# A graph-attention layer on one core: the first stage redone, with twelve sets of adjacency rows issued during the projection

## The chip, the cores and the metric

The kernel runs on one core of a Trainium2 chip. The time is device microseconds (us) of one execution, as the median of several runs. One further execution was profiled; rows and stretches below are from that one. TensorE (PE) multiplies, VectorE (DVE), ScalarE (ACT) and GpSimd (POOL) do elementwise work, SyncE (SP) only issues DMAs. PEld is TensorE's weight load.

## What is computed

```python
h  = relu(layernorm(x))                 # x: 8192 x 256, f32
Wh = h @ W + b                          # 8192 x 256
e  = leaky_relu((Wh @ a1)[:, None] + (Wh @ a2)[None, :], 0.2)
att = softmax(where(adj > 0, e, -9e15), axis=1)   # adj: 8192 x 8192, int32
out = x + att @ Wh
```

With s = Wh a1 and t = Wh a2, the exponential of leaky_relu(s_i + t_j) is the greater of two products of a row factor and a column factor. So the weight of a pair is max(q_i * r_j, sigma) times a column factor c_j that is multiplied into Wh, and the adjacency limits it from above (`min` with a number made of the adjacency bits). The softmax denominator is one more column of Wh.

## The kernel before

**Tiling.** The 8192 rows of x are 64 blocks of 128. The output is made in NS = 8 rows of R = 1,024 output rows ("row 0" to "row 7"). Each row takes all 8192 columns in NK = 32 units of two blocks. Eight PSUM banks `acc` hold the 8 x 128 output rows, and a unit is 2 x 8 x 3 fp16 products of 128 x 257 (high times high, high times low, low times high parts; `part`, L636).

**First stage.** SyncE loads the parameters and then x into `x_in` in four groups of 16 blocks (L194). For each group VectorE takes statistics (`stats`, L408; aggregation L414), adds eps (L416), ScalarE takes the square root (L272), and VectorE inverts (L418) and makes the shift (L419). Then, block by block: ScalarE normalises into a two-buffer `h` (`normalise`, L280), TensorE transposes it (L604), ScalarE copies the transpose out of PSUM (`copy_hT`, L287), TensorE projects (L612; two more columns of W, made of W times a at L395, give s and t), VectorE adds the bias and stores Wh with s and t in the tile `X` (`add_bias`, L426), and GpSimd sums Wh over the blocks (`add_wh`, L244). In between GpSimd issues the first 8 sets of adjacency rows, a set after every fourth block.

**Adjacency.** A set is four DMAs of a quadrant of 32 partitions (`load_adj`, L251, on GpSimd's queue, int32 cast to uint8). There are R8 = 12 slots; set n waits for the transpose of set n - 12 (`s_T`). VectorE turns a set with one transpose (L457); 8 sets are a chunk of 8 units.

**Between projection and row 0.** VectorE takes the largest and smallest t (L460 to L463), GpSimd reduces them over the partitions (L258) and then goes on to sets 8 and later; VectorE makes exponents (L468 to L475), ScalarE the exponentials (L347 to L351), VectorE scales q (L484). SyncE stores q to HBM in four DMAs, waits for all four, and loads row 0 of q into every partition:

```python
            sp.wait_ge(s_qn, 1)
            for q in range(NQ):
                sp.dma_start(q_store[q], ...).then_inc(s_qst, 16)
            sp.wait_ge(s_qst, 16 * NQ)
            load_q(0)
            sp.wait_ge(s_mean, 1)
```

**A unit of the main part.** ScalarE makes two products q * r_j (`product`, L323), VectorE takes max and min (`weights`, L508), ScalarE the high parts in fp16 (`high`, L338), VectorE the low parts (`low`, L515), TensorE multiplies. Four units are in flight (RING = 4). In row 0 alone, ScalarE and VectorE also split each block of Wh, scaled by c_j, into high and low halves (`x_high`, L344; `x_low`, L521), in place in `X`. ScalarE does four products of row 0 before the first high part. `first_units` waits for two units, then goes bank by bank, opening each bank with a product with the column mean of Wh (L647). At the end of a row `finish` (L529, L532) divides and adds x, and SyncE stores.

The order on each engine is written out by hand, and every engine runs its own list in order; semaphores tie them together.

Of the kernel before, what the change touches and what calls it, by code (L numbers as in the profile page):

```python
# [12 lines left out]
RMAX = bass.bass_isa.ReduceOp.max  # L13
RADD = bass.bass_isa.ReduceOp.add

P = 128
# [8 lines left out]
TINY = 2.0 ** -100  # L25


def gat_layer(nc, x, adj, W_w, W_b, a, out):

# [25 lines left out]
    KF = F // P  # L55
    XG = Y
    AHEAD = 2
# [11 lines left out]
    with ctx:  # L69
# [6 lines left out]

        X = sb("X", [P, NB + AHEAD, F2], F32)
        X16 = X[:, :, :].bitcast(F16).rearrange("p b (k f) -> p b k f", k=2)
        wh_s_t = X[:, AHEAD:AHEAD + NB, :]
        wh = X[:, AHEAD:AHEAD + NB, 0:F]  # L80
        wh_one = X[:, AHEAD:AHEAD + NB, 0:F1]
        s_in = X[:, AHEAD:AHEAD + NB, F]
        t_in = X[:, AHEAD:AHEAD + NB, F1]

# [5 lines left out]
        r_j = sb("r_j", [P, NB], F32)  # L90
        c_j = sb("c_j", [P, NB], F32)
        sigma = sb("sigma", [P, 1], F32)
# [12 lines left out]
        h = xr[:, 0, 0:2, :]  # L105
        hT = xr[:, 0, 2:4, :]
        prod = h[:, 0, :]
        a_row = hT
# [3 lines left out]
        wh_sum = xr[:, 1, 0:2, :]  # L112
        small = xr[:, 1, 2:4, :].rearrange("p k f -> p (k f)")
        st = small[:, 0:96].rearrange("p (n v) -> p n v", n=XG)
        mv = small[:, 96:128].rearrange("p (n v) -> p n v", n=XG)
        rstd = small[:, 128:192]
        shift = small[:, 192:256]
        ones = small[:, 256:384]
        mean_hi = small[:, 384:512].bitcast(F16)
# [5 lines left out]
        sc = sb("sc", [P, 16], F32)  # L125
# [3 lines left out]
        ps_wh = [acc[:, 2, :], acc[:, 3, :]]  # L129
        ps_tot = acc[:, 4, :]  # L130

        s_par = sem("params_loaded")
        s_x = [sem(f"x_loaded{k}") for k in range(NB // XG)]
        s_rows = [sem(f"adj_loaded{k}") for k in range(R8)]
        s_qst = sem("q_stored")
        s_q = sem("q_loaded")
        s_xr = [sem(f"x_rows_loaded{k}") for k in range(2)]
        s_out = [sem(f"out_stored{k}") for k in range(2)]

        s_ident = sem("ident_step")  # L140
        s_wsq = sem("w_squares_in_partition")
        s_wsq_all = sem("w_squares_summed")
        s_wnorm = sem("w_norm_ready")
        s_var = sem("variance_ready")
        s_std = sem("std_ready")
        s_norm = sem("norm_factors_ready")
        s_ext = sem("extremes_ready")
        s_top = sem("extremes_of_all_ready")
# [3 lines left out]
        s_c = sem("column_factors_ready")  # L152
        s_tot = sem("sum_wh_in_psum")
        s_mean = sem("mean_wh_ready")
        s_chain = sem("vector_chain")
        s_bn = sem("bn_step")

        s_h = sem("h_ready")
        s_ht = sem("h_transposed")
        s_hT = sem("hT_ready")  # L160
        s_whp = sem("wh_in_psum")
        s_wh = sem("wh_ready")
        s_sum = sem("wh_summed")
        s_xhi = sem("x_hi_ready")
        s_X = sem("X_ready")
# [18 lines left out]
        def _(sp):  # L184
            for k in range(KF):
                sp.dma_start(Wx[:, k, 0:F], W_w[k * P:(k + 1) * P, :]).then_inc(s_par, 16)
            sp.dma_start(bias[:, 0:F], W_b.rearrange("(o f) -> o f", o=1).broadcast_to([P, F])).then_inc(s_par, 16)
# [3 lines left out]
            for k in range(NC):  # L191
                xk = x_in[:, k * Y:(k + 1) * Y, :].rearrange("p (w e) f -> p w (e f)", e=4)
                for q in range(NQ):
                    sp.dma_start(xk[QP * q:QP * (q + 1)], x_cols[q, k]).then_inc(s_x[k], 16)  # L194
# [9 lines left out]

            sp.wait_ge(s_qn, 1)
            for q in range(NQ):
# [22 lines left out]
        @block.gpsimd  # L229
        def _(pool):  # L230
            nc.gpsimd.memset(ident[:, :], 0.0).then_inc(s_ident, 1)
            pool.wait_ge(s_ident, 1)
            nc.gpsimd.affine_select(out=ident[:, :], in_=ident[:, :], compare_op=ALU.not_equal, fill=1.0, base=0,
                                    pattern=[[-1, P]], channel_multiplier=1).then_inc(s_ident, 1)
            pool.wait_ge(s_wsq, 1)
            nc.gpsimd.partition_all_reduce(sc[:, 1:2], sc[:, 0:1], P, RADD).then_inc(s_wsq_all, 1)

            def add_wh(b, k, first):
                pool.wait_ge(s_wh, b + 1)
                if first:  # L240
                    nc.gpsimd.tensor_copy(wh_sum[:, k, :], wh[:, b, :]).then_inc(s_sum, 1)
                else:
                    pool.wait_ge(s_sum, b - 1)
                    nc.gpsimd.tensor_tensor(wh_sum[:, k, :], wh_sum[:, k, :], wh[:, b, :], ALU.add).then_inc(s_sum, 1)  # L244
            def load_adj(n):

                if n >= R8:
                    pool.wait_ge(s_T, n - R8 + 1)
                s, k, m = n // NSET, n % NSET // SETS, n % SETS
                for q in range(NQ):  # L250
                    pool.dma_start(rows8[QP * q:QP * (q + 1), n % R8], adj_v[s, m, k, q]).then_inc(s_rows[n % R8], 16)  # L251

            for b in range(NB):
                add_wh(b, b % 2, b < 2)
                if b >= SETS and b % 4 == 0 and b // 4 - 2 < SETS:
                    load_adj(b // 4 - 2)
            pool.wait_ge(s_ext, 1)
            nc.gpsimd.partition_all_reduce(top[:, :], ext[:, :], P, RMAX).then_inc(s_top, 1)  # L258
            for n in range(SETS, NSET * NS):
                load_adj(n)  # L260

        @block.scalar
        def _(act):
            act.wait_ge(s_par, 16 * (KF + 3))
            nc.scalar.activation(h, Wx[:, :, 0:F], ACT.Square, accum_out=sc[:, 0:1]).then_inc(s_wsq, 1)
            act.wait_ge(s_wsq_all, 1)
            nc.scalar.activation(sc[:, 2:3], sc[:, 1:2], ACT.Sqrt, scale=float(F)).then_inc(s_wnorm, 1)

            def std(k):
                act.wait_ge(s_var, k + 1)  # L270
                v = rstd[:, k * XG:(k + 1) * XG]
                nc.scalar.activation(v, v, ACT.Sqrt).then_inc(s_std, 1)  # L272

            std(0)
            act.wait_ge(s_norm, 1)

            def normalise(b, k, first):
                if not first:
                    act.wait_ge(s_ht, b - 1)
                nc.scalar.activation(h[:, k, :], x_in[:, b, :], ACT.Relu, scale=rstd[:, bass.ds(b, 1)],  # L280
                                     bias=shift[:, bass.ds(b, 1)]).then_inc(s_h, 1)

            def copy_hT(b, k, first):
                act.wait_ge(s_ht, b + 1)
                if not first:
                    act.wait_ge(s_whp, b - 1)
# [417 lines left out]
```

## Time and profile before

| | |
|---|---|
| median of 3 runs | 1554.79 us (1554.2 to 1555.71) |
| the profiled execution | 1553.04 us, its span 1551.1 |
| TensorE, busy share of the span | 93% |
| VectorE | 92% |
| ScalarE | 72% |
| GpSimd | 38% |
| granted TensorE clock, mean | 0.982 |

The span is the time from the first to the last instruction in the profile. A row of a timeline gives the start, the time, the engine, the line in the kernel, the operation, what it writes and reads, and how many were merged (x4). "Idle before" names what released the engine. A granted clock of 1.00 is 2.4 GHz, 0.50 is 1.2 GHz. The clock is given per stretch. Matmuls are pipelined, so a busy TensorE isn't a TensorE at its peak.

### The profile page before, as it was taken

The numbers are of one execution on the slowest core, as the hardware profiler recorded it, in microseconds if no ns is written. First come the engines' busy times: TensorE is split into PE (matmuls) and PEld (weight loads), VectorE is DVE, ScalarE is ACT, GpSimd is POOL, SyncE is SP. The second block draws the span as 40 slices with busy tenths as digits, with TensorE's granted clock in tenths as the row PEclk, the third lists the DMA queues.
The fourth block names the chain that finished last, engine by engine and source line by source line (L and its number), as shares of the span: only waits on it lengthen the run. The fifth ranks groups of instructions, "written<-read, shape, count | busy, mean of one in ns | idle before, by whom it ended". The sixth has DMA issues, their size and how long they took to land.

```text
span 1551.1 us, 30326 instructions
## 1 busy us (share of the span) xinstructions
PE 1448.3 (93%) x12740; PEld 1258.0 (81%) x12740; DVE 1425.4 (92%) x1155; ACT 1110.9 (72%) x975; POOL 593.7 (38%) x1096
## 2 busy tenths in 40 slices
PE   2880899979999999999999999999999999999998
PEld 2760787768888888888888888888888888888887
DVE  4654999999999999999999999999999999999994
ACT  3664788877777677768777777768777777767771
POOL 0866433334444344334434343434343434423000
PEclk9995899999999999999999999999999999999999
DMA  9719866668776777778777877778767877676000
GB/s 195 80 14 118 65 44 48 44 60 103 56 55 59 100 56 52 52 84 81 52 52 63 100 54 53 60 99 57 54 49 62 103 55 53 49 97 50 1 1 28
DMA packets 170768, 99.07 MB, mean 64 GB/s; under 512 B 19472, under 2 KB 167568, under 8 KB 170640
## 3 DMA queue, kind: packets, MB, share of 16 engines
q0 software_dynamic: 147456, 67.17, 61.2%
q1 hardware_dynamic: 23184, 30.05, 7.1%
q8 instruction: 97, 1.59, 0.4%
q14 instruction: 31, 0.25, 0.1%
HBM read 290.06 MB, written 8.42 MB: 192 GB/s over the span
## 4 chain that ended last, share of the span: by engine, by line
PE 82%; DVE 12%; issue 2%; DMA 2%; ACT 1%; SPq 0%; DVEq 0%; POOL 0%; ACTq 0%; POOLq 0%
PE acc L636 77%; DVE work L515 4%; PE acc L612 3%; DVE work L508 3%; DVE X L521 1%; DMA work<-in_x 1%; PE acc L604 1%; DMA q_rows<-q_j 1%; DVE adj_cols L457 1%; DVE xr L408 1%; ACT work L323 1%; PE acc L647 0%; DMA work<-q_rows 0%; DVE xr L414 0%; ACT work L338 0%
## 5 line engine op out<-in xcount | busy, mean ns | idle before, releaser
L636 PE MATMUL acc<-X,work 128*128 128x257 f16 x12288 | 1372.6, 273 | 12.9 <-DVE work L515 12.9
L636 PEld LDWEIGHTS acc<-X,work 128*128 128x128 f16 x12288 | 1189.4, 97 | 188.8 <-DVE work L515 16.8
L251 POOL DMA_DIRECT2D adj_rows<-in_adj x1024 | 550.8, 545 | 776.0 <-DVE adj_cols L457 752.5
L338 ACT ACTIVATE work<-work 128x2048 f16<-128x2048 f32 x256 | 487.6, 1907 | 276.7 <-PE acc L636 274.0
L508 DVE SCALAR_TENSOR_TENSOR work<-work,sigma,adj_cols 128x2048 f32<-128x2048 f32 x256 | 594.6, 2323 | 20.8 <-issue 17.3
L515 DVE SCALAR_TENSOR_TENSOR work<-work 128x2048 f16<-128x2048 f32 x256 | 584.9, 2285 | 29.3 <-ACT work L338 29.2
L323 ACT ACTIVATE work<-work,r_j 128x1024 f32<-128x1024 f32 x256 | 278.1, 1134 | 28.3 <-DMA work<-q_rows 17.9
L323 ACT ACTIVATE work<-q_odd,r_j 128x1024 f32<-128x1024 f32 x256 | 278.5, 1135 | 23.3 <-DVE work L515 23.3
L457 DVE STREAM_TRANSPOSE adj_cols<-adj_rows 128x512 int32<-128x512 int32 x256 | 176.0, 699 | 0.0
L612 PE MATMUL acc<-q_odd,xr 128*128 128x258 f32 x256 | 68.8, 393 | 9.0 <-DVE X L426 9.0
L647 PE MATMUL acc<-mean_wh,tiny 128*128 128x257 f16 x64 | 17.7, 276 | 47.1 <-DVE work L515 46.5
L426 DVE TENSOR_TENSOR X<-acc,q_odd 128x258 f32<-128x258 f32 (+1 forms) x64 | 26.9, 423 | 34.4 <-PE acc L612 32.3
L612 PEld LDWEIGHTS acc<-q_odd,xr 128*128 128x128 f32 x256 | 45.2, 197 | 14.0 <-DVE X L426 9.7
L344 ACT ACTIVATE X<-X,c_j 128x257 f16<-128x257 f32 x64 | 29.1, 504 | 30.8 <-DVE X L521 29.1
L604 PE MATMUL acc<-q_odd,xr 128*128 128x128 f32 x128 | 25.2, 282 | 27.2 <-ACT xr L280 27.2
L244 POOL TENSOR_TENSOR xr<-xr,X 128x256 f32<-128x256 f32 x62 | 41.2, 683 | 19.9 <-DVE X L426 19.7
L604 PEld LDWEIGHTS acc<-q_odd,xr 128*128 128x128 f32 x128 | 18.3, 145 | 34.2 <-issue 27.5
L647 PEld LDWEIGHTS acc<-mean_wh,tiny 128*128 128x128 bf16 x64 | 6.2, 96 | 48.7 <-issue 47.7
L280 ACT ACTIVATE xr<-work,xr 128x256 f32 (+1 forms) x64 | 38.3, 600 | 6.0 <-issue 5.2
L287 ACT COPY xr<-acc 128x256 f32<-128x256 f32 x64 | 23.7, 370 | 16.4 <-PE acc L604 12.1
L521 DVE SCALAR_TENSOR_TENSOR X<-X,c_j 128x257 f16<-128x257 f32 x64 | 28.0, 480 | 0.0
L532 DVE SCALAR_TENSOR_TENSOR xr<-acc,rden,xr 128x256 f32<-128x256 f32 x64 | 26.5, 477 | 0.6
(60 smaller groups left out, 54.0 us busy)
## 6 DMA issues: line engine op xcount, KB each, us to landing
adj_rows<-in_adj POOLq DMA_DIRECT2D x1024, 64.0 KB, 3.7
work<-in_x SPq DMA_DIRECT2D x16, 512.0 KB, 21.4
xr<-in_x SPq DMA_DIRECT2D x16, 512.0 KB, 4.0
out<-xr SPq DMA_DIRECT2D x16, 512.0 KB, 3.8
work<-q_rows SPq DMA_DIRECT2D x4, 512.0 KB, 5.7
q_odd<-q_rows SPq DMA_DIRECT2D x4, 512.0 KB, 5.4
q_odd<-in_L_gnn_W_w SPq DMA_DIRECT2D x2, 128.0 KB, 2.1
xr<-in_L_gnn_a SPq DMA_DIRECT2D x2, 128.0 KB, 6.1
```

The costliest lines, as they stand in the source:

```text
L244: nc.gpsimd.tensor_tensor(wh_sum[:, k, :], wh_sum[:, k, :], wh[:, b, :], ALU.add).then_inc(s_sum, 1)
L251: pool.dma_start(rows8[QP * q:QP * (q + 1), n % R8], adj_v[s, m, k, q]).then_inc(s_rows[n % R8], 16)
L280: nc.scalar.activation(h[:, k, :], x_in[:, b, :], ACT.Relu, scale=rstd[:, bass.ds(b, 1)], bias=shift[:, bass.ds(b, 1)]).then_inc(s_h, 1)
L323: ins = nc.scalar.mul(Wt[:, i % RING, e, :], q_bc[s % 2], r_j[:, 2 * k + e:2 * k + e + 1])
L338: nc.scalar.mul(Et[:, at:at + 2, 0, :], Wt[:, i % RING], SCALE).then_inc(s_H, 1)
L457: nc.vector.transpose(rows.rearrange("p w (q r) -> p q w r", q=SQ), rows8[:, n % R8].bitcast(I32).rearrange("p q (w c) -> p q w c", w=CW)) ...
L508: nc.vector.scalar_tensor_tensor(out=slot, in0=slot, scalar=sigma[:, 0:1], in1=edges, op0=ALU.max, op1=ALU.min).then_inc(s_M, 1)
L515: nc.vector.scalar_tensor_tensor(out=Et[:, at:at + 2, 1, :], in0=Wt[:, i % RING], scalar=SCALE, in1=Et[:, at:at + 2, 0, :], op0=ALU.mult, ...
L521: nc.vector.scalar_tensor_tensor(out=X16[:, b, 1, 0:F1], in0=wh_one[:, b, :], scalar=c_j[:, b:b + 1], in1=X16[:, b, 0, 0:F1], op0=ALU.mult ...
L604: ins = nc.tensor.transpose(ps_hT[k][:, c * P:(c + 1) * P], h[:, k, c * P:(c + 1) * P], ident)
L612: ins = nc.tensor.matmul(ps_wh[k][:, 0:F2], hT[:, k, c * P:(c + 1) * P], Wx[:, c, :], start=(c == 0), stop=(c == KF - 1))
L636: return nc.tensor.matmul(acc[:, m, 0:F1], Et[:, 2 * (k % RING) + e, 1 if n == 2 else 0, m * P:(m + 1) * P], X16[:, 2 * k + e, 1 if n == 1 ...
```

## The change

The diff rewrites the first stage and leaves the unit of the main part as it was.

- x comes in seven groups (4, 4, 8, 8, 8, 16, 16 blocks), the first ahead of the parameters. The inverse square root is made on VectorE, from the bits of the number and three rounds of Newton's method. The steps are dealt out over the pairs of blocks (`STATS_AT`, `norms`).
- `normalise` works in place in `x_in`. The odd blocks' transposes are copied out by VectorE, the even ones' by ScalarE.
- Wh is no longer stored. It stays in one of six PSUM banks, and `x_high` and `x_low` split it from there during the projection. Since the largest t isn't known yet, each pair of blocks is scaled by its own greater t (`greater_t`, `column_exps`, `scale_columns`); r_j and sigma (now one value for each pair) are corrected for that later.
- The bias is left out of Wh and is added to x's rows by an accumulating DMA (`add_bias` on GpSimd's queue, 16 in all), before `finish` uses them.
- GpSimd adds h instead of Wh, and TensorE makes the mean of Wh from the sum. The reductions over partitions are products on TensorE.
- All twelve sets of adjacency rows that have a slot are issued during the projection, a quadrant after each add from block 8 on. Four sets are transposed in the last four pairs.
- SyncE stores the first half of the first quarter of q, loads row 0 of q, and stores the rest behind it.
- Row 0: ScalarE begins with two products instead of four, and TensorE starts after one unit.

The diff, cut to its core:

```diff
+    GROUPS = [(0, 0, 1, 0), (0, 1, 2, 4), (0, 2, 4, 8), (1, 0, 2, Y), (1, 2, 4, Y + 8), (2, 0, 4, 2 * Y), (3, 0, 4, 3 * Y)]
+    STATS_AT = [None, None, (0, 2), (2, 2), (5, 2), (8, 4), (14, 4)]
...
             sp.wait_ge(s_qn, 1)
-            for q in range(NQ):
-                sp.dma_start(q_store[q], q_j[QP * q:QP * (q + 1), :].rearrange("p (z e) -> p z e", e=4)).then_inc(s_qst, 16)
+            store_q(0, 0, NZ // 2, s_q0)
+            sp.wait_ge(s_q0, 16)
+            load_q(0)
+            store_q(0, NZ // 2, NZ, s_qst)
+            for q in range(1, NQ):
+                store_q(q, 0, NZ, s_qst)
             sp.wait_ge(s_qst, 16 * NQ)
-            load_q(0)
+            sp.wait_ge(s_X, NB)
             sp.wait_ge(s_mean, 1)
...
+            for b in range(1, NB):
+                add_h(b)
+                if EARLY <= b < EARLY + NQ * R8:
+                    load_quadrant(*divmod(b - EARLY, NQ))
+            for n in range(R8, NSET * NS):
                 load_adj(n)
+                if n % NSET == 2 * R8 + 3:
+                    for half in range(2):
+                        add_bias(n // NSET, half)
...
+            for p in range(PAIRS + 1):
+                if p >= 2:
+                    x_high(2 * p - 4)
+                    x_high(2 * p - 3)
+                if 2 * p + 3 < NB:
+                    normalise(2 * p + 3)
+                if p >= 1:
+                    column_exps(p - 1)
+                if 2 * p + 2 < NB:
+                    copy_hT(2 * p + 2)
+                if 2 * p + 4 < NB:
+                    normalise(2 * p + 4)
...
-            for i in range(RING):
-                product(0, i)
+            product(0, 0)
+            product(0, 1)
             high(0, 0)
+            product(0, 2)
+            high(0, 1)
+            product(0, 3)
+            product(0, 4)
...
+            def root(g):
+                b, n = of_group(g)
+                a, y = newt[:, 0:n], rstd[:, b:b + n]
+                step(nc.vector.scalar_tensor_tensor(out=a, in0=y, scalar=-0.5, in1=y, op0=ALU.mult, op1=ALU.mult))
+                step(nc.vector.tensor_tensor(a, a, var[:, 0:n], ALU.mult))
+                step(nc.vector.scalar_tensor_tensor(out=y, in0=a, scalar=1.5, in1=y, op0=ALU.add, op1=ALU.mult))
...
+            def norms(p, place):
+                for g in range(2, len(GROUPS)):
+                    at, turns = STATS_AT[g]
+                    n = p - at
+                    if place == 0 and 0 <= n < turns:
+                        stats(g, 4 * n, 4 * n + 4)
+                    if place == 0 and n == turns:
+                        variance(g)
+                    if place == 1 and n == turns:
+                        guess(g)
+                        root(g)
+                    if place == 2 and n == turns:
+                        root(g)
+                    if place == 3 and n == turns:
+                        root(g)
+                        shifts(g)
+
+            def pair(p):
+                copy_hT(2 * p + 1)
+                if p >= 1:
+                    read_s_t(p - 1)
+                norms(p, 0)
+                if p >= 1:
+                    greater_t(p - 1)
+                norms(p, 1)
+                if p >= 2:
+                    x_low(2 * p - 4)
+                norms(p, 2)
+                if p >= 2:
+                    x_low(2 * p - 3)
+                norms(p, 3)
+                if p >= 1:
+                    scale_columns(p - 1)
...
+            first_groups()
+            for p in range(PAIRS):
+                pair(p)
+                if p == 0:
+                    bounds()
+                if p >= PAIRS - TURNED:
+                    transpose(0, p - PAIRS + TURNED)
...
+            def project(b):
+                k = b % 2
+                pe.wait_ge(s_hT[k], b // 2 + 1)
+                if b >= WH:
+                    pe.wait_ge(s_X, b - WH + 1)
...
+            for m in range(M):
+                start(m)
+            unit(0, 0)
+            unit(0, 1).then_inc(s_pe, 1)
```

`first_groups` does the statistics and factors of groups 0 and 1 and the four products of W with a. `variance` is the aggregation and the addition of eps, `guess` one operation on the bits, `shifts` one more. `bounds` makes the power of two that scales all columns, from the norm of W.

## Rows read from the trace of the kernel before

**Rows 1.** Stretches: us; PE, PEld, DVE, ACT, POOL busy; PEclk, DMA share, GB/s.

```profile
27.10:111.10 84.00, 74.28 (x384) 61.81 (x384) 49.16 (x170) 58.83 (x131) 58.56 (x95) 1.00 0.59 73
...
121.30:141.00 19.70, 0.00 (x0) 0.00 (x0) 4.44 (x13) 0.92 (x3) 19.70 (x38) 0.50 1.23 106
```

**Rows 2.** Busy time of output rows 1 to 6, columns as in rows 1.

```profile
350.00:1374.84 1024.84, 1024.84 (x9265) 896.08 (x9265) 1004.52 (x640) 765.50 (x576) 414.21 (x771) 1.00 0.75 65
```

**Rows 3.** Timeline of TensorE: the products that open row 0 and row 1.

```profile
159.49 0.38 PE L647 MATMUL acc<-mean_wh,tiny 128*128 128x257 f16 x1 [46.49 <-DVE work L515]
...
350.00 0.27 PE L647 MATMUL acc<-mean_wh,tiny 128*128 128x257 f16 x1 [0.57 <-DVE xr L532]
```

**Rows 4.** Timeline of VectorE: one unit of row 0.

```profile
165.79 2.31 DVE L508 SCALAR_TENSOR_TENSOR work<-work,sigma,adj_cols 128x2048 f32<-128x2048 f32 x1
168.02 0.88 DVE L521 SCALAR_TENSOR_TENSOR X<-X,c_j 128x257 f16<-128x257 f32 x2
168.81 2.28 DVE L515 SCALAR_TENSOR_TENSOR work<-work 128x2048 f16<-128x2048 f32 x1
171.01 0.70 DVE L457 STREAM_TRANSPOSE adj_cols<-adj_rows 128x512 int32<-128x512 int32 x1
171.64 2.31 DVE L508 SCALAR_TENSOR_TENSOR work<-work,sigma,adj_cols 128x2048 f32<-128x2048 f32 x1
```

**Rows 5.** The chain that ended last, from 111 to 160 us: start, time, what.

```profile
112.06 5.90 issue
123.00 11.79 DMA q_rows<-q_j
134.81 6.10 DMA work<-q_rows
141.00 8.42 ACT work L323 x8
```

**Rows 6.** DMA issues on the page: count, size, median us from issue to landing.

```profile
xr<-in_x SPq DMA_DIRECT2D x16, 512.0 KB, 4.0
...
q_odd<-in_L_gnn_W_w SPq DMA_DIRECT2D x2, 128.0 KB, 2.1
xr<-in_L_gnn_a SPq DMA_DIRECT2D x2, 128.0 KB, 6.1
```

**Rows 7.** Landings of the q stores (L207), then of the x loads (L194).

```profile
DMA to landing us min/median/max: 5.5/8.3/11.8
...
DMA to landing us min/median/max: 8.3/21.4/30.1
```

**Rows 8.** Timeline: single operations of the first stage, several merged in a row.

```profile
26.42 1.09 ACT L280 ACTIVATE xr<-work,xr 128x256 f32<-128x256 f32 x2 [0.53 <-DVE xr L419]
...
40.01 1.39 DVE L408 BATCH_NORM_STATS2 xr<-work 128x6 f32<-128x256 f32 x4
...
41.05 0.37 ACT L287 COPY xr<-acc 128x256 f32<-128x256 f32 x1
...
41.44 1.17 DVE L414 BATCH_NORM_AGGREGATE xr<-xr 128x2 f32<-128x6 f32 x16
...
44.56 0.76 DVE L426 TENSOR_TENSOR X<-acc,q_odd 128x258 f32 x2 [0.34 <-DVE xr L419]
...
50.82 2.17 POOL L251 DMA_DIRECT2D adj_rows<-in_adj  x4
53.00 2.61 POOL L244 TENSOR_TENSOR xr<-xr,X 128x256 f32<-128x256 f32 x4
...
122.17 0.91 ACT L344 ACTIVATE X<-X,c_j 128x257 f16<-128x257 f32 x2 [1.62 <-DVE c_j L487]
```

**Rows 9.** Small VectorE operations by line: ns minimum/median/maximum, first and last start.

```profile
L416 DVE TENSOR_SCALAR xr<-xr x4: 175/482/1005, 25.5 to 84.4; 128x16 f32<-128x16 f32 x4
...
L419 DVE SCALAR_TENSOR_TENSOR xr<-xr x4: 175/176/706, 26.2 to 85.6; 128x16 f32<-128x16 f32 x4
```

**Rows 10.** Timeline of ScalarE: the one table load before the exponentials.

```profile
109.16 1.28 ACT L347 ACT_TABLE_LOAD   x1
```

More of the change, by code:

```diff
@@ L269, in std @@
[L269 to L281, printed above, removed]
@@ L284, in copy_hT @@
+            def copy_hT(b):
                 act.wait_ge(s_ht, b + 1)
-                if not first:
+                if b >= 2:
                     act.wait_ge(s_whp, b - 1)
-                nc.scalar.copy(hT[:, k, :], ps_hT[k][:, 0:F]).then_inc(s_hT, 1)
-            normalise(0, 0, True)
-            normalise(1, 1, True)
-            copy_hT(0, 0, True)
-            normalise(2, 0, False)
-            copy_hT(1, 1, True)
-            def pairs(lo, hi):
-                with act.Fori(lo, hi) as pair:
-                    for k in range(2):
-                        normalise(2 * pair + k + 1, (k + 1) % 2, False)
-                        copy_hT(2 * pair + k, k, False)
@@ L301, in _ @@
[L301 to L312 removed]
+                nc.scalar.copy(hT[:, 0, :], ps_hT[0][:, 0:F]).then_inc(s_hT[0], 1)
@@ L398, in _ @@
-            for n in range(2):
-                step(nc.vector.tensor_tensor_reduce(out=prod, in0=bias[:, 0:F], in1=a_row[:, n, :],
-                                                    scale=1.0, scalar=0.0, op0=ALU.mult, op1=ALU.add,
-                                                    accum_out=bias[:, F + n:F + n + 1]))
-            step(nc.vector.memset(ones, 1.0))
-            step(nc.vector.memset(tiny[:, :], TINY))
-            step(nc.vector.memset(mean[:, :], 0.0))
-            step(nc.vector.tensor_reduce(sc[:, 3:4], bias[:, 0:F], AX.X, ALU.max, apply_absolute_value=True))
@@ new lines, in variance, with guess @@
+            def variance(g):
+                b, n = of_group(g)
+                dve.wait_ge(s_bn, b + n)
+                for i in range(n):
+                    ins = nc.vector.bn_aggr(mv[:, i, :], st[:, i, :])
+                step(ins)
+                step(nc.vector.tensor_scalar(var[:, 0:n], mv[:, 0:n, 1], EPS, None, ALU.add))
+            def guess(g):
+                b, n = of_group(g)
+                step(nc.vector.tensor_scalar(rstd[:, b:b + n].bitcast(I32), var[:, 0:n].bitcast(I32), -0.5, RSQRT_SEED, ALU.mult, ALU.add))
@@ new lines, in _ @@
+            greater_t(PAIRS - 1)
+            dve.wait_ge(s_bias, 16)
+            for n in range(2):
+                ins = nc.vector.tensor_tensor_reduce(out=X[:, NB - 1 - n, 0:F], in0=bias[:, 0:F], in1=a_row[:, n, :],
+                                                     scale=1.0, scalar=0.0, op0=ALU.mult, op1=ALU.add,
+                                                     accum_out=bias[:, F + n:F + n + 1])
+            step(ins)
+            step(nc.vector.tensor_tensor(sc[:, 24:25], bias[:, F:F + 1], bias[:, F + 1:F + 2], ALU.add))
@@ new lines, in _ @@
+            for e in range(2):
+                ins = nc.vector.tensor_tensor(r_2[:, :, e], r_2[:, :, e], t_fac, ALU.mult)
+            ins.then_inc(s_rf, 1)
+            dve.wait_ge(s_rf, 1)
+            x_low(NB - 3)
+            x_low(NB - 2)
+            x_low(NB - 1)
+            dve.wait_ge(s_col, 1)
+            nc.vector.tensor_scalar(hb, ps_hb[:, 0:F], 1.0 / N, None, ALU.mult).then_inc(s_hb, 1)
+            dve.wait_ge(s_c, PAIRS)
+            step(nc.vector.tensor_copy(X16[:, :, 0, F], c_j[:, :]))
```

494 lines of the change are left out of this document (268 added, 226 removed).

## The prediction

> **What bounds the kernel now.** I read the profile in this order: the page, then busy time by stretches, then the start times of the products that open each row of 1,024 output rows, then the vector engine's timeline inside row 0, and last the chain of work between the projection and the first main product.
>
> The page shows TensorE busy for 93% of the span and VectorE for 92%. That average says nothing of a first stage, so I cut the span where the row openers stand [rows 3]. Row 0 starts at 159.5 us and row 1 at 350.0, so row 0 lasts 190.5. The next six rows take 1024.84 us together, 170.8 each, with TensorE busy without a gap at a granted clock of 1.00 [rows 2]. The last row and its tail take what is left of the span, 176.3. So the span is 159.5 + 190.5 + 1024.8 + 176.3 = 1551.1 us. The six middle rows and the tail run the same instructions after the change, on a full TensorE; only the first two terms are open.
>
> Row 0 is 19.7 us longer than the others because VectorE bounds it. Its unit (two blocks of 128 columns) goes from 165.79 to 171.64, 5.85 us, of which `x_low` (L521) takes 0.79 from start to start [rows 4]. Without it the unit would be 5.06, under TensorE's 170.8 / 32 = 5.34.
>
> The first 159.5 us are three pieces: up to 27.1 loads and the first normalisation; 84.0 of projection, one block in 1.31 us [rows 1]; then 48.4 with nothing on TensorE but the column sum. That last piece is a chain [rows 5]: 5.9 us before GpSimd's reduction runs, 11.8 for the q values to land in HBM, 6.1 for q row 0 to come back, 8.4 for eight products on ScalarE, then weights and low parts.
>
> **The change, part by part, on the path.**
>
> *Start.* Group 0 of x is now 4 blocks instead of 16 and is issued first. Landing: between 4.6 us (issues done at 2.5, plus the 2.1 of the weight load) and 11.4 (issue at 3.1 plus the lowest landing of x, 8.3) [rows 6, 7]; I take 7, nearer the small load. Then four statistics (1.4), their aggregation (0.4) and 12 dependent small steps, as the square root is now a guess and three rounds on VectorE: at 0.175 each and 0.03 between [rows 9], 2.5. That is 11.3. The four products of W with a, 0.43 each by the nearest row [rows 8], end at 13.0; `a` itself lands near 4.2 + 6.1 = 10.3 [rows 6]. The second group costs the same 4.3, and the bound of W's norm some 0.7. The pair loop starts at 18.
>
> *Pair loop.* VectorE, per pair: `copy_hT` 0.38 (as L426, two in 0.76), two `x_low` 0.88, three tiny operations 0.5, so 1.75. ScalarE, per pair: two `normalise` 1.09, one copy 0.37, two `x_high` 0.91, and a tiny exp that I put within the overlap of their ends, so 2.4 [rows 4, 8]. TensorE needs at most 74.3 us for all pairs [rows 1], 2.3 each, and lies under both. By `STATS_AT`, 14 pairs carry four statistics (1.39): 1.75 + 1.39 = 3.14, VectorE-bound, 44.0. Five groups end in an aggregation and 12 small steps: 3.1 for 8 blocks, 3.7 for 16 (1.17 for the aggregation), so 16.7, and four of them stand in pairs without statistics, 7.0. The other 14 pairs are ScalarE's, 33.6; the four transposes of adjacency (0.62 each) fit in their vector slack. Pairs 0 and 1 lack `x_low` and more, -2.3, and `bounds()` adds 1. Sum 100.0, so the projection ends at 118; before, it ended at 111.1. So this piece does more work and ends later, although it starts earlier.
>
> The sum lets nothing of a pair overlap the next, too much by some us. Against that stands GpSimd, which adds h in SBUF all along: beside such adds L416 took 0.175 to 1.005 us and L419 up to 0.706 [rows 9]. The excess over 0.175 is 2.0 us in eight executions, 0.25 each, but an add holds up one step of a chain, not each: two adds at some 0.4 in each of five chains is 4 us. I let the two cancel. Bounds: 110 and 126. The Trainium skill (SBUF — State Buffer, "Who interferes with whom") says that a VectorE operation with two SBUF inputs, or in a two-port mode, and a GpSimd operation shut each other out for a whole instruction; this speaks against the change, whose rounds are such operations. The rows agree in kind. By the rule at its worst, every one of 60 steps waits for a whole add of 0.65 [rows 8], 39 us; by the rows' mean 15 at most.
>
> The 12 sets of adjacency rows are issued one quadrant after each add from block 8 on. An add costs GpSimd 0.65 us and a quadrant 0.54 [rows 8], so a block costs it 1.2 against a cadence of 1.2 to 1.5. Nothing on the path waits for it but the mean, which is not due for another 15 us. They are hidden; uncovered, the lag would cost below 5.
>
> *From the projection to q.* Before, this stretch was 10.2 us (111.1 to 121.3), of which 5.9 stood before the reduction [rows 5]. Two TensorE round trips near 0.5 replace it; an `x_low` (0.4) and two products with the bias (0.9) are added, less some waits: 5.2. q is ready at 123.2, about where it was. Bounds 4 and 8.
>
> *q out and back.* Only an eighth of q has to land before row 0 of it is loaded. Before, each of the four stores took 5.5 to 11.8 us, with a DMA share of 1.23 from 48 adjacency DMAs then issued in one go [rows 1, 7]. Now only sets 12 to 15 are in flight, freed one by one by the transposes in the last four pairs, and the store has half the packets of one of the four. Bounds 2.1 and 11.8; I take 4.5, close under the lowest store. The load took 6.1; a load of that size elsewhere 4.0 [rows 5, 6]. Sets 16 to 19 are issued beside it, so 5.7. q is back at 133.4.
>
> *To the first product.* Two multiplications at 1.05 instead of eight in 8.4 [rows 5], two weights at 2.3 and one low part at 2.2 [rows 4]: TensorE starts at 133.4 + 0.1 + 2.1 + 6.8 = 142.4 instead of 159.5, since it now begins after one unit, with X ready. What VectorE owes before that (three `x_low`, four transposes, the mean: some 6 us) lies inside the 10 us of the store and load; if q came back at once, it would cost about 3.
>
> *Row 0.* `x_high` and `x_low` are gone from it, so TensorE bounds it at 170.8, and I add 0.8 for the start at half clock (0.50 in the stretch before [rows 1]): 171.6 instead of 190.5.
>
> *The rest.* Sigma by column pair, the bias added by 16 accumulating DMAs of 512 KB on GpSimd's queue. The trace has none. From below nothing; from above, eight times an adjacency DMA: 4.4 us of GpSimd and 30 of transfer. They stand in the queue ahead of loads that have eleven transposes (over 55 us) of lead, and `finish` needs them over 80 us later. I take 0; 0 to 2.
>
> Sum: row 1 starts at 142.4 + 171.6 = 314.0 instead of 350.0, 36.0 earlier: 17.1 from the stage, 18.9 from row 0. The profiled execution took 1553.04, 1.9 outside its span, so 1517.0; the median of the runs is 1.75 above it, so 1518.8.
>
> **The rivals.** (1) *Row 0 gives nothing back*: something else late in VectorE or ScalarE keeps it near 190. VectorE would have 0.28 us in hand per unit, which is little; but the middle rows hold 170.8 with the same operations. -17: 1538.
>
> (2) *TensorE falls to half clock in the projection*, the case on the other side. It was busy 74.3 of 84.0 us before at 1.00 [rows 1]; now 74 of 100. If the clock is 0.50 throughout, its work is 148 us against 100, 48 more, and the time 1567. It decides once the projection is 36 us longer, at three quarters of it at half clock. Against it: the stops are short, and the clock stayed at 1.00 over those of before.
>
> (3) *ScalarE reloads its function table at each exp*. Before, exp stood outside the loop; a load is 1.28 us [rows 10]. Now 32 exps alternate with Relu. Two loads a pair are 82 us on ScalarE's 74: 156 against 100, 1575. Before, Relu ran after the square root and the multiplication after exp without a load, which speaks against. The Trainium skill (ScalarE: Activation LUTs, "Table sets: the hidden batching unit") says that relu lies in every set, so none would be loaded; the case depends on that.
>
> (4) *The q transfers stay as slow as they were* because adjacency traffic still fills the DMA engines: store 11.8, load 6.1, 8 us later: 1527. Inside the range.
>
> **How the numbers follow.** My case with (4) has 0.82, (1) 0.06, (2) 0.05, (3) 0.03, and 0.04 is for a wait that I don't see, half of it ending slower or equal. The case's own bounds: low, -8 in the projection, -2.4 and -1.7 in the transfers, about 1507; high, +8 and +7.3, about 1534; stretched to 1537 to take in part of (1). A measurement here can tell 0.2%, 3 us. Faster 0.91, same 0.02, slower 0.07.
>
> **What would show it.** Row 1's opener near 314 and row 0 at 171 to 172 with TensorE full; projection ending near 118, with pairs of 3.1 us where statistics stand and 2.4 where not, clock 1.00; one exp-table load in all; the first q store landing in about 4.5 us and TensorE's first part near 142. Wrong would be: many table loads, a clock of 0.5 before 118, small vector steps of 0.5 us and more, or a row 0 over 180.

## The result and the profile after

| | before | after |
|---|---|---|
| median of the runs | 1555.1 us (4 runs) | 1521.06 us (1520.91 to 1521.31, 4 runs) |
| ratio, 95% interval | | 0.9779 (0.9765 to 0.9793) |
| profiled execution, its span | 1553.04, 1551.1 | 1521.0, 1519.2 |
| projection ends | 111.1 | 118.8 |
| q ready | 121.3 | 123.7 |
| first main product | 159.5 | 145.5 |
| row 1 opens | 350.0 | 317.9 |

The change makes the kernel 34 us faster. By the profiles, row 1 opens 32.1 us sooner: 14.0 us at the start of row 0, 18.1 in row 0, and nothing after it. The projection is taken to end where the last t is copied (L460 before, the last L480 after). Line numbers below are those of each kernel's own listing.

TensorE's timeline, the answer to [rows 3]. Row 0 has its eight openers before the wait now, so it begins with the first part:

```profile
145.49 4.91 PE L789 MATMUL acc<-X,work 128*128 128x257 f16 x22 [13.37 <-DVE work L662]
...
317.88 0.27 PE L793 MATMUL acc<-mean_wh,tiny 128*128 128x257 f16 x1
```

Busy time by stretch, for the loop over pairs, row 0 and rows 1 to 6; the columns are those of [rows 1, 2]:

```profile
16.50:118.80 102.30, 83.87 (x376) 64.15 (x376) 92.17 (x368) 69.35 (x183) 71.20 (x114) 0.93 0.76 91
145.49:317.88 172.39, 172.39 (x1536) 149.87 (x1537) 171.94 (x107) 137.66 (x103) 75.29 (x137) 0.99 0.78 70
317.88:1342.84 1024.96, 1024.96 (x9266) 896.45 (x9264) 1003.78 (x637) 765.54 (x576) 430.47 (x782) 1.00 0.80 72
```

Row 0 keeps TensorE full, and the six middle rows take what they took (1024.96 against 1024.84). VectorE's timeline of a unit of row 0, against [rows 4], shows 5.06 us from 151.04 to 156.10, with `x_low` gone:

```profile
151.04 2.31 DVE L655 SCALAR_TENSOR_TENSOR work<-work,sigma,adj_cols 128x2048 f32<-128x2048 f32 x1
153.27 2.28 DVE L662 SCALAR_TENSOR_TENSOR work<-work 128x2048 f16<-128x2048 f32 x1
155.47 0.70 DVE L580 STREAM_TRANSPOSE adj_cols<-adj_rows 128x512 int32<-128x512 int32 x1
156.10 2.31 DVE L655 SCALAR_TENSOR_TENSOR work<-work,sigma,adj_cols 128x2048 f32<-128x2048 f32 x1
```

The chain between q and row 0, against [rows 5]:

```profile
123.74 6.28 DMA q_rows<-q_j
...
130.03 6.28 DMA work<-q_rows
...
136.40 2.19 ACT work L362 x2
```

And GpSimd's timeline, which says why the store took 6.28 us and not the 4.5 that I took:

```profile
115.32 0.73 POOL L279 TENSOR_TENSOR h_sum<-h_sum,work 128x256 f32<-128x256 f32 x1 [0.49 <-ACT work L317]
115.99 8.64 POOL L284 DMA_DIRECT2D adj_rows<-in_adj  x16
127.21 8.58 POOL L284 DMA_DIRECT2D adj_rows<-in_adj  x16 [2.59 <-DVE adj_cols L580]
```

Sets 12 to 15 aren't issued one by one as the last four pairs free their slots. In GpSimd's list they stand behind the last addition of h, so all sixteen DMAs go out from 116.0 to 124.6, right ahead of the q store.

Small operations by line, against [rows 9]: `scale_columns` (L491, two elements for each partition), `greater_t` (L485, one element), and the last step of a round (L462):

```profile
L491 DVE TENSOR_SCALAR c_j<-c_j,sc x32: 210/228/933, 22.6 to 122.8; 128x2 f32<-128x2 f32 x32
...
L485 DVE TENSOR_SCALAR xr<-xr x32: 188/213/216, 22.0 to 119.4; 128x1 f32<-128x1 f32 x32
...
L462 DVE SCALAR_TENSOR_TENSOR xr<-xr x21: 161/167/1018, 7.5 to 85.8; 128x8 f32<-128x8 f32 x9, 128x4 f32<-128x4 f32 x6, 128x16 f32<-128x16 f32 x6
```

The groups of instructions hold one table load in all, so the exponentials (L329) and the normalisations with Relu (L317) ran from the same table:

```profile
L310 ACT ACT_TABLE_LOAD x1 | 1.3, 1283 | 0.7 <-PEq L845 0.7
```

Last, TensorE alone by stretch (busy, granted clock, DMA share, GB/s). The clock did fall in the projection:

```profile
86.00:88.00 2.00, 1.15 (x3) 0.50 0.51 32
88.00:90.00 2.00, 2.00 (x7) 0.50 0.10 2
90.00:92.00 2.00, 2.00 (x7) 0.50 0.82 50
92.00:94.00 2.00, 2.00 (x11) 0.86 0.69 46
94.00:100.00 6.00, 6.00 (x35) 1.00 0.73 44
```

### The profile page after: what moved, and what is told of

The parts are those of the page before. It is cut to its first block, busy times and chain, and to the rows that moved or that the text cites. A ratio compares the mean times of both kernels' runs of the same rounds, so it can differ in the third digit from the quotient of the medians.

```text
span 1519.2 us, 30042 instructions
## 1 busy us (share of the span) xinstructions
PE 1461.2 (96%) x12750; PEld 1265.1 (83%) x12750; DVE 1443.0 (95%) x1300; ACT 1099.8 (72%) x970; POOL 618.7 (41%) x1109
## 4 chain that ended last, share of the span: by engine, by line
PE 91%; DVE 5%; DMA 1%; issue 1%; ACT 1%; SPq 0%; DVEq 0%; ACTq 0%
PE acc L789 90%; PE acc L751 1%; DVE xr L437 1%; DVE X L495 1%; DVE xr L475 1%; DVE c_j L491 0%; DMA work<-q_rows 0%; DMA q_rows<-q_j 0%; PE acc L793 0%; DMA work<-in_x 0%; DVE xr L447 0%; ACT X L334 0%; DVE xr L462 0%; DVE xr L461 0%; DVE xr L460 0%
## 5 line engine op out<-in xcount | busy, mean ns | idle before, releaser
L751 PEld LDWEIGHTS acc<-q_odd,xr 128*128 128x128 f32 x256 | 48.5, 211 | 31.2 <-ACT xr L325 12.3
L279 POOL TENSOR_TENSOR h_sum<-h_sum,work 128x256 f32<-128x256 f32 x62 | 45.5, 733 | 34.9 <-ACT work L317 34.3
L317 ACT ACTIVATE work<-work,xr 128x256 f32<-128x256 f32 x64 | 38.1, 600 | 5.6 <-DVE xr L466 5.6
L742 PE MATMUL acc<-q_odd,work 128*128 128x128 f32 x128 | 26.6, 294 | 10.9 <-ACT work L317 10.9
L334 ACT ACTIVATE X<-acc,c_j 128x256 f16<-128x256 f32 x64 | 26.6, 468 | 13.7 <-DVE c_j L491 13.7
L742 PEld LDWEIGHTS acc<-q_odd,work 128*128 128x128 f32 x128 | 18.5, 152 | 20.0 <-issue 10.9
L495 DVE SCALAR_TENSOR_TENSOR X<-acc,c_j,X 128x256 f16<-128x256 f32 x64 | 28.2, 476 | 0.4
L437 DVE BATCH_NORM_STATS2 xr<-work 128x6 f32<-128x256 f32 x64 | 22.3, 411 | 5.1 <-DMA work<-in_x 5.1
L294 POOL DMA_DIRECT2D xr<-in_L_gnn_W_b x16 | 21.3, 1616 | 1.0 <-issue 1.0
L329 ACT ACTIVATE c_j<-xr 128x2 f32<-128x2 f32 x32 | 9.4, 294 | 16.4 <-DVE xr L485 16.3
## 6 DMA issues: line engine op xcount, KB each, us to landing
work<-in_x SPq DMA_DIRECT2D x8, 512.0 KB, 23.7
```

Source lines behind the costliest of these rows:

```text
L279: nc.gpsimd.tensor_tensor(h_sum[:, :], first, x_in[:, b, :], ALU.add).then_inc(s_hsum, 1)
L317: nc.scalar.activation(x_in[:, b, :], x_in[:, b, :], ACT.Relu, scale=rstd[:, b:b + 1], bias=shift[:, b:b + 1]).then_inc(s_h, 1)
L495: nc.vector.scalar_tensor_tensor(out=X16[:, b, 1, 0:F], in0=ps_wh[:, b % WH, 0:F], scalar=c_j[:, b:b + 1], in1=X16[:, b, 0, 0:F], op0=ALU. ...
L742: ins = nc.tensor.transpose(ps_hT[k][:, c * P:(c + 1) * P], x_in[:, b, c * P:(c + 1) * P], ident)
L751: ins = nc.tensor.matmul(ps_wh[:, b % WH, 0:F2], hT[:, k, c * P:(c + 1) * P], Wx[:, c, :], start=(c == 0), stop=(c == KF - 1))
```

## The experiments

All but one start from the changed kernel, 1521.06 us, run again beside the later ones at 1520.44 (e11). The kernel before, run beside each group, had medians of 1555.4 to 1556.81, so a difference of under 2 us between two experiments isn't firm; there the profiles say more. A pair of blocks is measured below from one `read_s_t` (L480) to the next, and the five pairs that end a group of x are those with an aggregation and the twelve small steps.

**e1: sets 12 and later held until row 0 of q is back.**

```diff
+            pool.wait_ge(s_q, 16)
             for n in range(R8, NSET * NS):
                 load_adj(n)
```

> GpSimd waits, before it issues adjacency set 12 (the first one that needs a freed slot), until row 0 of q is back in SBUF. In the changed kernel sets 12 to 15 are issued at 116.0 to 124.6 us, because they stand behind the last addition of h, and the q store (issued at 123.7) lands in 6.28 us, the load in another 6.28. Queue theory (these transfers are slow because of adjacency traffic in the DMA engines): store near 3, load near 4.5, TensorE starts 4 to 5 us before 145.5 and the time is 1516 to 1517. Latency theory (a store of 16-byte pieces and a broadcast of 512 KB take about 6 us each whatever else runs): no change, 1521. Supply theory (the held sets then come too late for the transposes of unit 4 and later): row 0 longer than 172.4 us, time 1521 or more.

1513.74 us, ratio to the kernel before 0.973 (0.9713 to 0.9746). SyncE's queue and ScalarE's first products:

```profile
122.31 0.31 SPq L236 DMA_DIRECT2D q_rows<-q_j  x1
123.99 0.34 SPq L227 DMA_DIRECT2D work<-q_rows  x1
...
128.89 4.26 ACT L363 ACTIVATE work<-work,r_j 128x1024 f32<-128x1024 f32 x4 [6.19 <-DMA work<-q_rows]
```

The store needs 1.7 us instead of 6.28 and the load 4.9 instead of 6.3. TensorE starts at 137.98, 7.5 earlier, of which 6.1 are these two. The other 1.4 is a projection that ended sooner; the hold begins behind the last addition and can't have caused it. Row 0 took 171.3, so the held sets were not missed. That the traffic slows the two transfers holds, and the latency theory falls. I had expected 4 to 5 us; it is 6.1 by the rows, and 7.3 by the medians.

**e2: all of q stored before row 0 is loaded.**

```diff
-            store_q(0, 0, NZ // 2, s_q0)
-            sp.wait_ge(s_q0, 16)
-            load_q(0)
-            store_q(0, NZ // 2, NZ, s_qst)
-            for q in range(1, NQ):
+            for q in range(NQ):
                 store_q(q, 0, NZ, s_qst)
             sp.wait_ge(s_qst, 16 * NQ)
+            load_q(0)
```

> All four q stores are issued and landed before row 0 of q is loaded, as in the kernel before; all else as changed. If storing only an eighth first is what shortened the wait (11.8 before, 6.28 after), the four stores take about 11 to 12 us and TensorE starts 5 to 6 us later, time 1526 to 1527. If the shorter wait came from less adjacency traffic alone, TensorE starts at most 2 us later, time 1521 to 1523.

1525.54 us, 4.5 slower, just under my 1526 to 1527; TensorE starts at 151.55, 6.1 later. SyncE's queue:

```profile
123.30 3.98 SPq L236 DMA_DIRECT2D q_rows<-q_j  x4
135.69 0.34 SPq L227 DMA_DIRECT2D work<-q_rows  x1
```

The four stores take 12.4 us, nearly the 13.5 from 121.3 to 134.8 of before the change. So the shorter store came from how much is waited for, and hardly from less adjacency traffic. The first of the four stores, twice as large as the one of the change, landed in 7.2 us, so not waiting for the other three is worth more than halving the first.

**e10: the same hold in the kernel before**, from set 8 on.

```diff
+            pool.wait_ge(s_q, 16)
             for n in range(SETS, NSET * NS):
                 load_adj(n)
```

> The kernel before with its adjacency sets from 8 on held until row 0 of q is back, the rest as it was. Queue theory: the four q stores land in 3 to 5 us instead of 11.8 and the load in about 5 instead of 6.1, so TensorE starts 8 to 10 us before 159.5; a row of the unchanged rest keeps its length: 1545 to 1547. If sets 8 to 11 then come too late for the first transposes of row 0, part of it is lost: 1548 to 1553.

1545.49 us against 1555.92 beside it, ratio 0.9932 (0.9916 to 0.9948). The load is issued 7.7 us after the first store, where I had expected 3 to 5, and its data are used 3.7 us later, from 133.12:

```profile
121.76 1.91 SPq L207 DMA_DIRECT2D q_rows<-q_j  x4
129.44 0.34 SPq L197 DMA_DIRECT2D work<-q_rows  x1
...
133.12 8.42 ACT L324 ACTIVATE work<-work,r_j 128x1024 f32<-128x1024 f32 x8 [9.59 <-DMA work<-q_rows]
```

TensorE starts at 151.62, 7.9 earlier, and row 1 opens at 341.80 instead of 350.0. By the medians it is 10.4 us; by these rows, one line gives the old kernel a quarter of what the whole change gave.

**e6: row 0's vector load put back.** Two operations of 252 elements per unit, into a tile that nobody reads.

```diff
             def low(g, i):
+                if g < NC:
+                    for e in range(2):
+                        if g or i:
+                            dve.wait_ge(s_extra, 2 * (NI * g + i) + e - 1)
+                        nc.vector.scalar_tensor_tensor(out=extra[:, e, :], in0=extra[:, 2, :], scalar=sigma[:, 0:1],
+                                                       in1=extra[:, 2, :], op0=ALU.mult, op1=ALU.subtract).then_inc(s_extra, 1)
                 dve.wait_ge(s_H, NI * g + i + 1)
```

> In the 32 units of row 0 VectorE does two more operations of 252 elements per unit, about what x_low cost there before (0.79 us for both); their result is not used. If the gain of row 0 came from taking x_low off VectorE, a unit takes about 5.06 + 0.79 = 5.85 us again and row 0 is 188 to 191 instead of 172.4: time 1536 to 1540. If it came from ScalarE's x_high or from the later start of the first chunk, row 0 stays under 176 and the time under 1525.

1544.75 us, 23.7 slower, more than my 15 to 19. TensorE starts at 145.90 and row 1 opens at 341.54, 195.6 later. The mechanism is the one expected (a unit is 5.88, from 234.41 to 240.29), but my number forgot that TensorE now starts one unit sooner: in the same measure the old row 0 was 190.5 plus a unit of 5.85, 196.4. ScalarE's `x_high` was not put back, so all of the old length comes from VectorE's part.

```profile
234.41 2.35 DVE L658 SCALAR_TENSOR_TENSOR work<-work,sigma,adj_cols 128x2048 f32<-128x2048 f32 x1
236.68 0.87 DVE L667 SCALAR_TENSOR_TENSOR extra<-extra,sigma 128x252 f32<-128x252 f32 x2
237.46 2.28 DVE L671 SCALAR_TENSOR_TENSOR work<-work 128x2048 f16<-128x2048 f32 x1
239.66 0.70 DVE L583 STREAM_TRANSPOSE adj_cols<-adj_rows 128x512 int32<-128x512 int32 x1
240.29 2.31 DVE L658 SCALAR_TENSOR_TENSOR work<-work,sigma,adj_cols 128x2048 f32<-128x2048 f32 x1
```

**e3: GpSimd adds 2 of the 256 columns of h.**

```diff
-                first = x_in[:, 0, :] if b == 1 else h_sum[:, :]
-                nc.gpsimd.tensor_tensor(h_sum[:, :], first, x_in[:, b, :], ALU.add).then_inc(s_hsum, 1)
+                first = x_in[:, 0, 0:2] if b == 1 else h_sum[:, 0:2]
+                nc.gpsimd.tensor_tensor(h_sum[:, 0:2], first, x_in[:, b, 0:2], ALU.add).then_inc(s_hsum, 1)
```

> GpSimd adds 2 of 256 columns of h for each block (the column mean is left out but for two columns). Port theory (VectorE's small operations wait while a GpSimd addition holds a shared SBUF port): scale_columns stays near 0.23 us instead of up to 0.93, the three rounds near 0.17 instead of up to 1.02, and the projection ends 4 to 8 us before 118.8; time 1513 to 1517. As GpSimd is then no longer behind, sets 12 to 15 are also issued earlier and the q store lands sooner, 1 to 3 us more. Rival (those waits hide in VectorE's slack): projection end within 1 us of 118.8, time 1519 to 1521.

1512.09 us, 9.0 faster, just under my 1513 to 1517. The same two lines of small operations as above, first `scale_columns`, then the round's last step, never wait:

```profile
L494 DVE TENSOR_SCALAR c_j<-c_j,sc x32: 219/228/231, 22.4 to 113.8; 128x2 f32<-128x2 f32 x32
...
L465 DVE SCALAR_TENSOR_TENSOR xr<-xr x21: 161/166/176, 7.7 to 80.6; 128x8 f32<-128x8 f32 x9, 128x4 f32<-128x4 f32 x6, 128x16 f32<-128x16 f32 x6
```

The q store goes out at 114.79 instead of 123.74. It still takes 6.0, since the sixteen DMAs again stand just ahead of it. The projection ends at 109.6, 9.1 sooner. Not all of that is waits for additions. The five pairs that end a group take 25.3 us instead of 29.8, and the eight pairs from 93.6 to 112.5 us take 17.5 instead of 19.0. TensorE's clock stayed at 1.00 from 34 to 106 us in this profile, and the remaining 3 are about what that alone gives (2.8, e7 below). Against e7, whose clock also stayed up, e3's projection ends 6.3 us sooner, and that is the better price of the waits.

**e8: `scale_columns` as two operations of one element.**

```diff
-                nc.vector.tensor_scalar(c, c, sc[:, 8:9], 2.0, ALU.mult, ALU.mult).then_inc(s_c, 1)
+                nc.vector.tensor_scalar(c[:, 0:1], c[:, 0:1], sc[:, 8:9], 2.0, ALU.mult, ALU.mult)
+                nc.vector.tensor_scalar(c[:, 1:2], c[:, 1:2], sc[:, 8:9], 2.0, ALU.mult, ALU.mult).then_inc(s_c, 1)
```

> scale_columns multiplies its two columns in two operations of one element for each partition instead of one of two elements. In the changed kernel the operation of two took 0.21 to 0.93 us beside GpSimd's additions, while greater_t, one element, never took more than 0.22. Mode theory (an even count lets the operation use both ports and so wait for GpSimd; one element cannot): both new operations stay near 0.2, pairs 23 to 28 lose up to 0.7 us each, the projection ends 2 to 4 us sooner and the time is 1517 to 1519. Rival (any multiplication in SBUF waits): two operations wait as much as one, 0.1 us more for each pair, 1521 to 1524.

1519.4 us, 1.7 faster than the base's first median and 1.0 than its second, so small beside the spread of its runs. What the profile shows is plain, though: neither half waits.

```profile
L491 DVE TENSOR_SCALAR c_j<-c_j,sc x32: 202/206/216, 22.1 to 121.7; 128x1 f32<-128x1 f32 x32
...
L492 DVE TENSOR_SCALAR c_j<-c_j,sc x32: 201/205/207, 22.2 to 121.9; 128x1 f32<-128x1 f32 x32
```

The extra operation costs each pair with statistics 0.1 us, which takes back part of it (2.86 instead of 2.74 from one `copy_hT` to the next). Late in the loop, where these pairs took 2.50 us in the changed kernel, they now take 2.19:

```profile
104.18 0.42 DVE L475 COPY xr<-acc 128x256 f32<-128x256 f32 x1 [0.22 <-PE acc L743]
...
106.37 0.42 DVE L475 COPY xr<-acc 128x256 f32<-128x256 f32 x1 [0.42 <-PE acc L743]
```

**e4: one round of the inverse square root instead of three** (a less exact normalisation).

```diff
-                for n in range(3):
+                for n in range(1):
                     root(0)
...
-                    if place == 2 and n == turns:
-                        root(g)
                     if place == 3 and n == turns:
-                        root(g)
                         shifts(g)
```

> One round of the inverse square root instead of three, so a less exact normalisation: 6 of 12 small vector steps fewer in each of seven groups. If VectorE bounds the pairs that end a group, five groups give 1.2 us each and the second of the first two another 1.2, with waits for GpSimd's additions saved on top: projection ends 6 to 9 us sooner, 1512 to 1515. If ScalarE or TensorE bounds them, under 2 us, 1519 to 1521.

1510.22 us, 10.8 faster and below my 1512 to 1515; q is out at 112.9. Six groups by six steps by 0.2 are 7.2. TensorE's clock stayed at 1.00 in this profile in the stretches where it had fallen (34 to 56 and 76 to 90 us), and e7, which only keeps the clock up, gets 2.8. The rest, about 1, is put down to waits saved with the steps; that is not shown.

**e7: TensorE's stops filled with spare products**, three before an even and two before an odd block in the five pairs that end a group.

```diff
+                if b % 2 == 0:
+                    pe.wait_ge(s_hT[k], b // 2 + 1)
+                    for c in range(FILL.get(b, 0)):
+                        nc.tensor.matmul(ps_hT[k][:, 0:F], ident, Wx[:, 0, 0:F], start=True, stop=True)
                 if b >= WH:
                     pe.wait_ge(s_X, b - WH + 1)
+                if b % 2 == 1:
+                    for c in range(FILL.get(b, 0)):
+                        nc.tensor.matmul(ps_wh[:, b % WH, 0:F], ident, Wx[:, 0, 0:F], start=True, stop=True)
+                    pe.wait_ge(s_hT[k], b // 2 + 1)
```

> TensorE does 3 (even block) and 2 (odd block) spare f32 products of 128x128x256 where it stood waiting in the changed kernel, in the five pairs that end a statistics group. Clock theory: the granted clock fell to 0.50 three times in the projection (near 38 to 41, 51 to 55 and 85 to 92 us) because TensorE stood still in those pairs; with the stops filled it stays at 1.00, and the pairs behind them need 2.2 us instead of up to 3.8: projection ends 3 to 5 us sooner, time 1516 to 1518. Rival (VectorE bounds these pairs, and the spare work is in the way): end at 118.8 or later, time 1521 to 1523.

1518.98 us (1518.04 to 1519.53), 1.5 to 2.1 faster, just above my 1516 to 1518. The clock stayed at 1.00 where it had been 0.66 in the changed kernel:

```profile
84.00:94.00 10.00, 9.98 (x50) 1.00 0.58 37
```

The projection ends 2.8 us sooner, less than the 3 to 5 expected.

The second profile of the changed kernel (e11) shows that the places of the drops change from one execution to the next. There the clock was 1.00 from 84 to 94 us, and the projection ended at 118.6, nearly as before. But it had fallen from 66 to 72 us instead:

```profile
66.00:72.00 6.00, 5.69 (x15) 0.50 0.44 29
```

TensorE's stops before that were the same in both. The first profile of the changed kernel, then e11:

```profile
64.91 1.11 PE L751 MATMUL acc<-q_odd,xr 128*128 128x258 f32 x4 [1.74 <-DVE X L495]
...
67.55 1.14 PE L751 MATMUL acc<-q_odd,xr 128*128 128x258 f32 x4 [1.31 <-DVE xr L475]
```

```profile
63.67 1.11 PE L751 MATMUL acc<-q_odd,xr 128*128 128x258 f32 x4 [1.73 <-DVE X L495]
...
66.31 2.09 PE L751 MATMUL acc<-q_odd,xr 128*128 128x258 f32 x4 [1.31 <-DVE xr L475]
```

Each of the two drops cost its own execution about 2.1 us where it lay: the two pairs at it took 7.1 against 4.9 in e11, and 6.9 against 4.7 in the first profile. So the drop at 86 to 92 us wasn't free. After it, though, the first profile ran three pairs at 2.19 us where e11 already ran at 2.50, which gave about half of it back.

**e5: no accumulating DMAs** (the bias is missing from the output).

> The 16 accumulating DMAs of the bias are left out (the bias is missing from the output), and finish waits for x's rows alone. They took GpSimd 1.34 to 1.91 us each and landed in 10.0 to 18.4. If they are hidden as predicted: 1520 to 1522, no difference. If they cost by contention: up to 0.5 us for each, 1513 to 1519.

1521.05 us, row 1 opening at 318.1 against 317.9: hidden, as predicted.

**e11: the changed kernel again, and e9 and e12: the edits together.** e9 is e1, e7 and e8 in one; e12 has two rounds instead of three besides.

> The changed kernel itself, on the same chip and in the same rounds as the two others, as their base: 1520 to 1522.

> Three edits together: adjacency sets from 12 on held until row 0 of q is back (alone 1513.7), spare products that fill TensorE's stops (alone 1519.0), scale_columns as two one-element operations (alone 1519.4), against 1521.1 for the changed kernel. If the gains are in different places they add: 7.3 + 2.1 + 1.7 = 11, time 1510. If the second and third win the same microseconds (both speed up the last pairs), 1512.

> The three edits of the run at 1510.6 and, besides, two rounds of the inverse square root instead of three. Going from three rounds to one gave 10.8 us, so if the small steps of VectorE are still on the path with TensorE's stops filled, one round fewer gives another 4 to 5 us: 1505 to 1507. If filling the stops has made TensorE the bound of those pairs, it gives under 2: 1509 to 1511.

e11: 1520.44 (1519.09 to 1521.71). e9: 1510.63, ratio to the kernel before 0.9711 (0.9698 to 0.9725). That is 3.1 beyond e1 alone, where e7 and e8 had promised 3.7. It lies between my two cases, 1510 and 1512, and doesn't decide between them. e12: 1506.93, ratio 0.9687 (0.9673 to 0.97), 3.7 below e9 and inside 1505 to 1507. Its projection ends at 111.5 against e9's 114.1, so the small steps were still on the path. It beats both kernels, by 14 us the changed one; its inverse square root is a round less exact.

## Why the prediction was right, and where it was off

**The total.** 1518 was forecast, 1521.06 measured, inside 1507 to 1537. Row 1 opens at 317.9 instead of 314.0. The mechanism held: row 0 became TensorE's and the stage in front of it shorter. But two of the four signs that I had named for being wrong did show, a clock of 0.50 before 118 us and small vector steps of 0.5 us and more, so the total is righter than its parts.

**Start and loop.** The loop over pairs began at 16.5 instead of 18, the projection ended at 118.8 instead of 118. That the sum came out is in part luck, since errors of opposite sign cancelled. A pair with statistics takes 2.74, not 3.14, because operations overlap; over fourteen pairs that is 5.6 us less. The five pairs that end a group took 29.8 against 26.8 in my sum, and the falls of TensorE's clock, for which the sum had nothing, cost 2.8 (e7). A pair without takes 2.19 at best, which is TensorE's pace (1.09 a block) and not ScalarE's 2.4. Late in the loop it takes 2.50, which is GpSimd's: three pairs in the first profile, six in e11. There an addition starts every 1.255 us, and the pairs lock to two of them. With the wait taken away they run at 2.19 again (e8). VectorE's and GpSimd's timelines:

```profile
101.37 0.93 DVE L491 TENSOR_SCALAR c_j<-c_j,sc 128x2 f32<-128x2 f32 x1
...
103.87 0.93 DVE L491 TENSOR_SCALAR c_j<-c_j,sc 128x2 f32<-128x2 f32 x1
```

```profile
101.52 0.74 POOL L279 TENSOR_TENSOR h_sum<-h_sum,work 128x256 f32<-128x256 f32 x1
102.20 0.57 POOL L284 DMA_DIRECT2D adj_rows<-in_adj  x1
102.78 0.74 POOL L279 TENSOR_TENSOR h_sum<-h_sum,work 128x256 f32<-128x256 f32 x1
```

The operation that starts at 101.37 ends at 102.30, 0.04 after the addition's end; the next one, at 103.87, ends 0.03 after its addition. Its recorded start lies before the addition's, so these rows alone don't show which waits for which; e3, in which only the additions shrink and no such operation is over 0.23 us, does. I let these waits and the overlap within pairs cancel at 4 us. The chains alone were priced well: the five pairs that end a group are 4.6 us shorter in e3. But "an add holds up one step of a chain" looked only at the 60 steps of the chains and left out `scale_columns`, which stands in every pair and late in the loop costs another 1.5 (2.5 in e7, where the pairs lock sooner).

With one element the same operation never waits (e8), with two it does, and `greater_t`, with one, never did. The rounds' operations, with two inputs in SBUF, wait too (up to 1.02 us for L462), and the same step doesn't in e3 (0.18). The Trainium skill says that a VectorE operation contends with GpSimd when it runs in a two-port mode or has two inputs in SBUF (SBUF — State Buffer, "Who interferes with whom"). The Trainium skill also says that an operation with one source takes the 2×_2P mode, a two-port one, if source and destination are in SBUF and their outermost dimensions of more than one element are both even or equal (VectorE: DVE Perf Modes, "What auto-detection actually checks"). The trace agrees with both for two elements. The case of one element isn't treated there; that it doesn't wait is what e8 shows.

**To q.** 5.2 us forecast, 4.9 measured (118.8 to 123.7).

**q out and back.** This is the term that was mis-sized: 4.5 and 5.7 forecast, 6.28 and 6.28 measured, 2.4 us of the 3.9 by which row 1 is late; q ready 0.5 late, row 0 with 0.8 and the first products with 0.2 are the rest. What failed is "freed one by one by the transposes in the last four pairs": I had looked at when the slots come free and not at what stands ahead of the loads in GpSimd's list. With the traffic gone (e1) the store is 1.7 us, under my lower bound of 2.1. Both halves of the argument were checked: the size (e2: 12.4 for four stores) and the traffic (e1, e10).

**Row 0.** 171.6 forecast, 172.4 measured. The split of the gain (17.1 in the stage, 18.9 in row 0) is less firm than it looked. Starting TensorE one unit sooner gains nothing while VectorE sets the pace, so in e6's measure taking VectorE's half of the splits out of row 0 is worth 23.7 us and the redone stage 10.

**Bias DMAs.** Taken at 0, measured at 0 (e5).

**The rivals.** (1) fell: row 0 is TensorE's. (2) happened for short stretches: the clock fell to 0.50 three times, near 38, 52 and 86 us, each time after TensorE had waited for VectorE in a pair that ends a group. In e11 it also fell three times, near 29, 49 and 66 us. A stop before a drop is not enough to bring it: those at 64.9 and 67.6 us had none behind them, and the same stops in e11 did. Together the drops cost the 2.8 us by which e7's projection ends sooner, 1.5 to 2.1 in the medians. (3) fell, with one table load. (4) was about half true: the load is as slow as it was (6.28 against 6.10), the store halved.

## What to carry to other kernels

A transfer that everything waits for should find the DMA queues empty. To see whether it does, read the issuing engine's own list, not the time at which its slots come free: a one-line hold was worth 6 us here and 8 in the old kernel by the start of row 0 (7 and 10 in the medians). A cheap helper on GpSimd can set the pace of VectorE, most of all through an operation that stands once in every turn of a loop. One profile isn't enough to say where TensorE's clock falls: a second one of the same kernel had drops up to 20 us away from those of the first. When work leaves a stage bounded by one engine, price it by that engine's time per unit and not by where the next stage starts.

## What was not expected of the hardware

A store of 256 pieces of 16 bytes landed in 1.7 us with the queues empty (e1) and in 6.28 with sixteen adjacency DMAs just issued. An accumulating DMA of 512 KB took 10.0 to 18.4 us to land and 1.34 to 1.91 us of GpSimd, where an adjacency DMA of 64 KB takes 0.55. An operation of VectorE on two elements took up to 0.93 us beside additions of 0.74, and as two operations on one element never more than 0.22. And a stretch of six microseconds of TensorE at half clock came in one execution at 86 us and in another at 66, behind the same stops, and cost about 2.1 us either way.
